# A slot of 57 columns for rows of 56: two gated 3x3 convolutions in float32 on one core

## The chip, the core and the metric

The kernel runs on one core of one Trainium2 chip. The metric is the device time of one execution in microseconds (us). The core has a matrix engine (TensorE, called PE in the profile, its weight loads PEld), a vector engine (DVE), a scalar engine (ACT), GpSimd (POOL), and SyncE (SP), which issues most of the DMAs. SBUF holds the operands, 128 partitions wide. PSUM takes the sums of TensorE, in 8 banks of 512 float32 columns.

## What is computed

The input x has 16 images, 64 channels, 56 by 56 pixels. A gated convolution with batch norm and ReLU is followed by a second one, and x is added before the last ReLU:

```python
def qconv_cg(x, w, theta):
    base = x.shape[1] // 4
    yp = conv3x3(x[:, :base], w[:, :base])        # padding 1 on each side
    yr = conv3x3(x[:, base:], w[:, base:])
    d = sigmoid(2.0 * (yp - theta[None, :, None, None]))
    return yp + d * yr
h = relu(bn(qconv_cg(x, w_a, theta_a), gamma_a, beta_a, mean_a, var_a))
h = bn(qconv_cg(h, w_b, theta_b), gamma_b, beta_b, mean_b, var_b)
return relu(x + h)
```

## The kernel before

**Layout.** Two neighbouring rows of an image share a slot: partition 2c+q holds channel c of the row of parity q. An image has 28 pairs of output rows and, since a pair of output rows reads four input rows, XS = 29 slots in the input layout. A row has W = 56 pixels, and in the tiles that TensorE reads (`x_hi`, `x_lo`, `h_hi`, `h_lo`, lines 112 to 115) it is stored with a zero on each side, so a slot takes PADW = 58 columns. The 3x3 taps become 2 slots by 3 shifts of dx = 0, 1 or 2 columns, six taps, each a 32 by 128 matrix for each of four groups of 16 channels.

**Precision.** A value is stored as a high part that TensorE's fast float32 format can hold and a low part, the rest. Each tap is done three times: high by high, high data by low weights, low data by high weights. That makes UNITS = 18 matmuls for each block and channel group.

**Blocks.** A block is BLK = 8 slots, N = 8 x 56 = 448 output columns of one PSUM bank. Convolution a has 56 blocks (the last of every seven takes 4 slots of each of two images, `a_slots`), convolution b has 58. `h_hi` and `h_lo` are rings of 116 slots, and two of the b blocks fall on the ring's end. After a lead of seven a blocks, `order` alternates b and a blocks, 114 in all.

**TensorE's work** is written out by hand in the loop at lines 324 to 362. A step issues one matmul for each of the channel groups 1, 2, 3, 0, in the order of the tuple. Each group sits in its own 32 rows of the array, so that the four run side by side. Groups 2, and 3 and 0, lag group 1 by 21 and 42 steps (LAG), so there are 18 x 114 + 42 = 2094 steps, the first and last 42 with fewer groups. Groups 1 to 3 add into one of five `yr` banks, group 0 into one of three `yp` banks (`yr_bank`, `yp_bank`, lines 175 to 179). `moving` (line 292) gives the data operand: eight rows of 56 columns out of slots of 58, shifted by dx. `unit` (line 312) issues the matmul on line 320.

**The other engines.** For each block ACT takes the sigmoid of the `yp` bank (line 403), DVE multiplies by the `yr` bank (503) and adds the `yp` bank (505). For an a block ACT then applies the batch norm and ReLU (409) and writes `h_hi` (414), DVE writes `h_lo` (510); for a b block DVE adds x (524) and ACT does the last ReLU (422). The splitting of x into `x_hi` (ACT, 378) and `x_lo` (DVE, 485) runs four a blocks ahead. At the start DVE and POOL write the zero columns and zero slots (lines 434, 263 and 266).

Of the kernel before, what the change touches and what calls it, by code (L numbers as in the profile page):

```python
# [10 lines left out]
P = 128  # L11
# [18 lines left out]
def gated_conv_pair_kernel(nc, x, w_a, theta_a, gamma_a, beta_a, mean_a, var_a,  # L30
# [4 lines left out]
    XS = SLOTS + 1  # L35
    PADW = W + 2
    N = BLK * W
    HALF = BLK // 2
    assert N <= BANK and SLOTS == 3 * BLK + HALF and (B * XS) % BLK == 0
    HRING = H_IMGS * XS  # L40
# [63 lines left out]
    with ExitStack() as ctx:  # L104
        def sb(name, shape, dt=F32):
            return ctx.enter_context(nc.sbuf_tensor(name, shape, dt))
# [4 lines left out]
        x32 = sb("x32", [P, X_IMGS * XS, W])  # L111
        x_hi = sb("x_hi", [P, XH_IMGS, XS, PADW], F32R)
        x_lo = sb("x_lo", [P, XH_IMGS, XS, PADW], F32R)
        h_hi = sb("h_hi", [P, HRING + 1, PADW], F32R)
        h_lo = sb("h_lo", [P, HRING + 1, PADW], F32R)
        mix = sb("mix", [P, MIX, N])
        rows_out = sb("rows_out", [P, OUT_IMGS * XS, W])
# [56 lines left out]

        def yr_bank(b):
            return psum[:, b % YR_BANKS, 0:N]

        def yp_bank(b):
            return psum[:, YR_BANKS + b % YP_BANKS, 0:N]

        def in_middle(tile, n):

            parts = a_slots(n)
            img, s, k = parts[0]
            t = (img % H_IMGS) * XS + 1 + s
            if len(parts) == 1:
                return tile[:, t:t + k, 1:1 + W]
            pair = tile[:, (img % H_IMGS) * XS:(img % H_IMGS + 2) * XS].rearrange("p (i s) w -> p i s w", i=2)
            return pair[:, :, 1 + s:1 + s + k, 1:1 + W]
# [12 lines left out]
        def split_chunk(tile, img, c):  # L202
            s0, s1 = CHUNKS[c]
            return tile[:, img % XH_IMGS, s0:s1, 1:1 + W]

# [46 lines left out]
        def _(pool):  # L252
# [9 lines left out]
            for n, t in enumerate((h_hi, h_lo)):  # L262
                nc.gpsimd.memset(t[:, :, 0:PADW:PADW - 1].bitcast(F32), 0.0).then_inc(hpads_zero, 1)

                pool.wait_ge(hpads_zero, 2 * n + 1)
                nc.gpsimd.memset(t[:, 0:HRING + 1:XS, :].bitcast(F32), 0.0).then_inc(hpads_zero, 1)

        @block.tensor
        def _(pe):
# [21 lines left out]

            def moving(blk, part, c, dx, g):
                kind, n = blk
                rows = slice(g * ROWS, (g + 1) * ROWS)
                if kind == "a":
                    tile = (x_hi, x_lo)[part]
                    parts = a_slots(n)
                    img, s, k = parts[0]
                    at = img % XH_IMGS
# [4 lines left out]
                t = BLK * n % HRING  # L304
                if t == HRING - HALF:
                    halves = tile[rows, c:c + HRING].rearrange("p (a b) w -> p a b w", b=HALF)
                    return halves[:, 0::HRING // HALF - 1, :, dx:dx + W]
# [57 lines left out]
        def _(act):  # L365
# [60 lines left out]
        def _(dve):  # L426
# [72 lines left out]
            for b, (kind, n) in enumerate(order):  # L499
                m = mix[:, b % MIX]  # L500
                dve.wait_ge(gate_ready, b + 1)
                dve.wait_ge(yr_ready, b + 1)
                nc.vector.tensor_tensor(m, m, yr_bank(b), ALU.mult).then_inc(gated_ready, 1)  # L503
                dve.wait_ge(gated_ready, b + 1)
                nc.vector.tensor_tensor(m, m, yp_bank(b), ALU.add).then_inc(mixed_ready, 1)  # L505
                if kind == "a":
# [46 lines left out]
```

## Time and profile before

| | us |
|---|---|
| median of 3 runs | 471.18 (470.81 to 471.21) |
| the profiled execution, its whole time | 471.88 |
| its span, from first to last instruction | 469.8 |
| PE busy, PEld busy | 452.7 (96%), 445.1 (95%) |
| DVE busy, ACT busy | 257.7 (55%), 219.6 (47%) |

Matmuls overlap one another, so PE's busy time says that some matmul was always under way, not how fast the columns flow. What tells this is the distance from the start of one matmul of a channel group to the start of the next of the same group. It is called a step below, and is read from the timeline.

### The profile page before, as it was taken

To read this page: it belongs to the slowest core of one execution; us is meant where nothing else is said; L and a number is where in the kernel's file an instruction comes from. 1 tells how busy PE (TensorE), PEld (TensorE's weight loads), DVE (VectorE), ACT (ScalarE), POOL (GpSimd) and SP (SyncE) were. 2 spreads that over 40 slices of the span, in tenths; PEclk is the share of its full clock that TensorE was granted. 3 is DMA by queue.
4 is the path that set the end of the run, shared out by engine and by line. 5 is a ranking of instruction groups with operands and counts; after the bars stand their busy time and mean duration, and the time that the engine had idled before them with its cause. 6 is when DMAs were issued, how large, how long until landed. Compare 5 with 4: busy or idle time off the path is not lost.

```text
span 469.8 us, 17744 instructions
## 1 busy us (share of the span) xinstructions
PE 452.7 (96%) x8233; PEld 445.1 (95%) x8233; DVE 257.7 (55%) x425; ACT 219.6 (47%) x346; POOL 7.0 (1%) x20
## 2 busy tenths in 40 slices
PE   3999999999999999999999999999999999999991
PEld 3999999999999999999999999999999999999991
DVE  8206655565655555565656555565656555545552
ACT  3226645454544545454544545454544545443331
POOL 5000000000000000000000000000000000000000
PEclk9999999999999999999999999999999999999996
DMA  9920000801726051070506151070333003030333
GB/s 176 218 43 3 3 3 3 137 3 26 116 44 96 3 119 22 8 135 19 122 3 117 26 117 24 4 139 1 81 62 71 3 1 71 3 66 6 72 72 68
DMA packets 116298, 27.13 MB, mean 58 GB/s; under 512 B 116096, under 2 KB 116096, under 8 KB 116224
## 3 DMA queue, kind: packets, MB, share of 16 engines
q1 hardware_dynamic: 115312, 25.86, 30.1%
q8 instruction: 65, 1.06, 1.0%
q10 hardware_dynamic: 592, 0.13, 0.1%
q14 instruction: 9, 0.07, 0.0%
q0 software_dynamic: 320, 0.00, 0.0%
HBM read 13.14 MB, written 12.85 MB: 55 GB/s over the span
## 4 chain that ended last, share of the span: by engine, by line
PE 96%; DVE 1%; ACT 1%; DMA 1%; issue 0%; ACTq 0%
PE acc L320 95%; DMA w_nat<-in_L_conv_w_a_dram 1%; DVE w_pad L441 0%; PE acc L281 0%; ACT L403 0%; ACT mix L403 0%; DVE w_lo L449 0%; ACT w_hi L369 0%; DVE rows_out L524 0%; ACT rows_out L422 0%; DVE mix L505 0%; DVE mix L503 0%; DVE x_lo L485 0%; ACT x_hi L378 0%; PE acc L289 0%
## 5 line engine op out<-in xcount | busy, mean ns | idle before, releaser
L320 PE MATMUL acc<-h_hi,w_hi 32*128 32x448 f32 x1392 | 226.7, 367 | 0.0
L320 PE MATMUL acc<-h_lo,w_hi 32*128 32x448 f32 x1392 | 226.6, 367 | 0.0
L320 PE MATMUL acc<-h_hi,w_lo 32*128 32x448 f32 x1392 | 226.5, 367 | 0.0
L320 PE MATMUL acc<-x_hi,w_hi 32*128 32x448 f32 x1344 | 224.5, 374 | 0.1
L320 PE MATMUL acc<-x_lo,w_hi 32*128 32x448 f32 x1344 | 224.2, 372 | 0.0
L320 PE MATMUL acc<-x_hi,w_lo 32*128 32x448 f32 x1344 | 224.1, 373 | 0.0
L320 PEld LDWEIGHTS acc<-h_hi,w_hi 32*128 32x128 f32 x1392 | 188.3, 184 | 1.2
L320 PEld LDWEIGHTS acc<-h_hi,w_lo 32*128 32x128 f32 x1392 | 188.2, 183 | 1.2
L320 PEld LDWEIGHTS acc<-h_lo,w_hi 32*128 32x128 f32 x1392 | 188.2, 183 | 1.0
L320 PEld LDWEIGHTS acc<-x_hi,w_hi 32*128 32x128 f32 x1344 | 185.9, 188 | 1.4 <-ACT x_hi L378 0.4
L320 PEld LDWEIGHTS acc<-x_hi,w_lo 32*128 32x128 f32 x1344 | 186.1, 188 | 1.0
L320 PEld LDWEIGHTS acc<-x_lo,w_hi 32*128 32x128 f32 x1344 | 185.9, 187 | 1.0
L503 DVE TENSOR_TENSOR mix<-mix,acc 128x448 f32<-128x448 f32 x114 | 70.8, 621 | 142.1 <-ACT mix L403 142.1
L422 ACT ACTIVATE rows_out<-rows_out,shift 128x448 f32<-128x448 f32 (+3 forms) x64 | 40.0, 634 | 120.4 <-DVE rows_out L524 120.4
L403 ACT ACTIVATE mix<-acc,gate_bias 128x448 f32<-128x448 f32 x114 | 72.3, 634 | 45.1 <-PE acc L320 44.4
L505 DVE TENSOR_TENSOR mix<-mix,acc 128x448 f32<-128x448 f32 x114 | 70.7, 620 | 3.9
L409 ACT ACTIVATE mix<-mix,shift,inv 128x448 f32<-128x448 f32 x56 | 42.7, 762 | 51.2 <-DVE mix L505 51.2
L510 DVE TENSOR_TENSOR h_lo<-mix,h_hi 128x448 fp32r<-128x448 f32 x56 | 35.1, 626 | 52.9 <-ACT h_hi L414 52.9
L524 DVE SCALAR_TENSOR_TENSOR rows_out<-mix,inv,x 128x448 f32<-128x448 f32 (+3 forms) x64 | 40.5, 641 | 2.0
L485 DVE TENSOR_TENSOR x_lo<-x,x_hi 128x504 fp32r<-128x504 f32 (+2 forms) x48 | 34.3, 715 | 1.3 <-ACT x_hi L378 1.3
L414 ACT ACTIVATE h_hi<-mix 128x448 fp32r<-128x448 f32 x56 | 32.5, 581 | 1.8
L378 ACT ACTIVATE x_hi<-x 128x504 fp32r<-128x504 f32 (+2 forms) x48 | 31.1, 649 | 2.5 <-DMA x<-in_x_dram 2.4
(47 smaller groups left out, 29.9 us busy)
## 6 DMA issues: line engine op xcount, KB each, us to landing
out_dram<-rows_out SPq DMA_DIRECT2D x32, 392.0 KB, 6.7
x<-in_x_dram SPq DMA_DIRECT2D x30, 392.0 KB, 5.5
x<-in_x_dram SPq DMA_DIRECT2D x1, 280.0 KB, 4.7
x<-in_x_dram SPq DMA_DIRECT2D x1, 266.0 KB, 5.1
w_nat<-in_L_conv_w_a_dram SPq DMA_DIRECT2D x1, 144.0 KB, 2.9
w_nat<-in_L_conv_w_b_dram SPq DMA_DIRECT2D x1, 144.0 KB, 4.0
x<-in_x_dram ACTq DMA_DIRECT2D x1, 126.0 KB, 3.0
x<-in_x_dram SPq DMA_DIRECT2D x1, 112.0 KB, 4.0
```

What stands on the lines that cost most here:

```text
L320: return pe.matmul(psum[:, bank, 0:N], w[g * ROWS:(g + 1) * ROWS, tap], moving(blk, part, c, dx, g), start=(u == 0 and g in (0, 1)), stop= ...
L378: nc.scalar.activation(split_chunk(x_hi, img, c), x_chunk(img, c), ACT.Copy).then_inc(xhi_ready, 1)
L403: nc.scalar.activation(mix[:, b % MIX], yp_bank(b), ACT.Sigmoid, scale=ALPHA, bias=gate_bias[:, k:k + 1]).then_inc(gate_ready, 1)
L409: nc.scalar.activation(mix[:, b % MIX], mix[:, b % MIX], ACT.Relu, scale=inv[:, 0:1], bias=shift[:, 0:1]).then_inc(h_ready, 1)
L414: nc.scalar.activation(in_middle(h_hi, n), as_block(mix[:, b % MIX], n), ACT.Copy).then_inc(hhi_ready, 1)
L422: last = nc.scalar.activation(rows, rows, ACT.Relu, bias=shift[:, 1:2])
L485: nc.vector.tensor_tensor(split_chunk(x_lo, img, c), x_chunk(img, c), split_chunk(x_hi, img, c).bitcast(F32), ALU.subtract).then_inc(xlo_r ...
L503: nc.vector.tensor_tensor(m, m, yr_bank(b), ALU.mult).then_inc(gated_ready, 1)
L505: nc.vector.tensor_tensor(m, m, yp_bank(b), ALU.add).then_inc(mixed_ready, 1)
L510: nc.vector.tensor_tensor(in_middle(h_lo, n), as_block(m, n), in_middle(h_hi, n).bitcast(F32), ALU.subtract).then_inc(hlo_ready, 1)
L524: last = nc.vector.scalar_tensor_tensor(rows_out[:, at:at + s, :].rearrange("p s w -> p (s w)"), m[:, col:col + s * W], inv[:, 1:2], x32[: ...
```

## The change

A row is now stored with one zero ahead of it, PITCH = 57 columns to a slot, and the zero ahead of the next slot's row serves as the one behind. A spare column stands ahead of the first slot and one behind the last. The data operand of a matmul is then SPAN = 8 x 57 = 456 columns in one run (for the blocks of two images and those on the ring's end, two runs of 228). The sums take 456 columns of a bank; column 0 of each slot's 57 is a sum that nobody needs, and ACT and DVE read the 56 behind it. The number of matmuls, their order, waits, banks and lags stay. Of the zeroing instructions, the one for two columns of each slot becomes one for the spare column and one for a column of each slot.

```diff
-    PADW = W + 2
-    N = BLK * W
+    PITCH = W + 1
+    SPAN = BLK * PITCH
...
+    def b_slots(m):
+        t = BLK * m % HRING
+        return [(0, HALF), (t, HALF)] if t == HRING - HALF else [(t, BLK)]
...
-        x_hi = sb("x_hi", [P, XH_IMGS, XS, PADW], F32R)
-        h_hi = sb("h_hi", [P, HRING + 1, PADW], F32R)
+        x_hi = sb("x_hi", [P, XH_IMGS, 1 + XS * PITCH + 1], F32R)
+        h_hi = sb("h_hi", [P, 1 + (HRING + 1) * PITCH + 1], F32R)
...
-        def yr_bank(b):
-            return psum[:, b % YR_BANKS, 0:N]
+        def slots(tile, t, k):
+            return tile[:, 1 + t * PITCH:1 + (t + k) * PITCH].rearrange("p (s w) -> p s w", w=PITCH)
+        def rows_of(bank):
+            return psum[:, bank, 0:SPAN].rearrange("p (s w) -> p s w", w=PITCH)[:, :, 1:]
...
-                    if len(parts) == 1:
-                        return tile[rows, at, s + c:s + c + k, dx:dx + W]
-                    return tile[rows, at:at + 2, s + c:s + c + k, dx:dx + W]
+                    at = (s + c) * PITCH + dx
+                    if len(parts) == 1:
+                        return tile[rows, img % XH_IMGS, at:at + SPAN]
+                    return tile[rows, img % XH_IMGS:img % XH_IMGS + 2, at:at + HALF * PITCH]
...
-                return tile[rows, t + c:t + c + BLK, dx:dx + W]
+                    return tile[rows, at:at + SPAN]
...
-                return pe.matmul(psum[:, bank, 0:N], w[g * ROWS:(g + 1) * ROWS, tap],
+                return pe.matmul(sums(bank, blk), w[g * ROWS:(g + 1) * ROWS, tap],
...
-                nc.scalar.activation(mix[:, b % MIX], yp_bank(b), ACT.Sigmoid, scale=ALPHA,
+                nc.scalar.activation(mix_rows(b), yp_rows(b), ACT.Sigmoid, scale=ALPHA,
...
-                last = nc.vector.memset(t[:, :, :, 0:PADW:PADW - 1].bitcast(F32), 0.0)
+                nc.vector.memset(t[:, :, 0].bitcast(F32), 0.0)
+                last = nc.vector.memset(t[:, :, 1::PITCH].bitcast(F32), 0.0)
...
-                nc.vector.tensor_tensor(m, m, yr_bank(b), ALU.mult).then_inc(gated_ready, 1)
+                nc.vector.tensor_tensor(mix_rows(b), mix_rows(b), yr_rows(b), ALU.mult).then_inc(gated_ready, 1)
```

## Rows read from the trace of the kernel before

**Rows 1.** The page, busy time of each engine: us (share of span) xinstructions.
```profile
PE 452.7 (96%) x8233; PEld 445.1 (95%) x8233; DVE 257.7 (55%) x425; ACT 219.6 (47%) x346; POOL 7.0 (1%) x20
```
**Rows 2.** The chain that ended last: start us, us, what.
```profile
10.63 21.57 PE acc L320 x126
...
34.71 425.35 PE acc L320 x7317
...
460.09 0.64 ACT mix L403
```
**Rows 3.** The page's costliest groups, line 320: busy us, mean ns of one.
```profile
L320 PE MATMUL acc<-h_hi,w_hi 32*128 32x448 f32 x1392 | 226.7, 367 | 0.0
...
L320 PEld LDWEIGHTS acc<-h_hi,w_hi 32*128 32x128 f32 x1392 | 188.3, 184 | 1.2
```
**Rows 4.** Timeline of PE, first stage, one group, then four: start us, us, engine, operation.
```profile
13.58 1.69 PE L320 MATMUL acc<-x_hi,w_lo 32*128 32x448 f32 x4
15.07 1.69 PE L320 MATMUL acc<-x_lo,w_hi 32*128 32x448 f32 x4
...
29.26 0.62 PE L320 MATMUL acc<-x_lo,w_hi 32*128 32x448 f32 x2
...
29.63 0.62 PE L320 MATMUL acc<-x_lo,w_hi 32*128 32x448 f32 x2
```
**Rows 5.** Two stretches: busy us (xinstructions) of each engine, granted clock, DMA, GB/s.
```profile
10.50:30.60 20.10, 20.10 (x118) 19.17 (x122) 4.52 (x16) 2.87 (x5) 0.00 (x0) 1.00 0.98 166
...
35.90:450.80 414.90, 414.90 (x7900) 409.79 (x7896) 236.77 (x381) 205.38 (x325) 0.00 (x0) 1.00 0.26 49
```
**Rows 6.** Timeline of PE near the end, three groups active, then two.
```profile
450.84 1.20 PE L320 MATMUL acc<-h_lo,w_hi 32*128 32x448 f32 x12
...
452.10 1.20 PE L320 MATMUL acc<-h_hi,w_hi 32*128 32x448 f32 x12
...
456.06 1.44 PE L320 MATMUL acc<-h_hi,w_hi 32*128 32x448 f32 x12
457.33 1.44 PE L320 MATMUL acc<-h_hi,w_lo 32*128 32x448 f32 x12
```
**Rows 7.** Timeline of PE in the middle, four steps on end, all four groups active.
```profile
200.16 0.38 PE L320 MATMUL acc<-h_hi,w_lo 32*128 32x448 f32 x2
...
200.37 0.38 PE L320 MATMUL acc<-h_hi,w_lo 32*128 32x448 f32 x2
...
200.58 0.38 PE L320 MATMUL acc<-h_hi,w_lo 32*128 32x448 f32 x2
...
200.78 0.38 PE L320 MATMUL acc<-h_hi,w_lo 32*128 32x448 f32 x2
```
**Rows 8.** Timeline of PE where group 1 begins its fifth block.
```profile
34.71 0.47 PE L320 MATMUL acc<-x_hi,w_hi 32*128 32x448 f32 x1
...
35.03 0.36 PE L320 MATMUL acc<-x_hi,w_hi 32*128 32x448 f32 x1
```
**Rows 9.** Timeline of the weight loads (PEld) there, with idle time before and its releaser.
```profile
34.71 0.18 PEld L320 LDWEIGHTS acc<-x_hi,w_hi 32*128 32x128 f32 x1 [0.45 <-ACT x_hi L378]
...
34.82 0.18 PEld L320 LDWEIGHTS acc<-x_hi,w_hi 32*128 32x128 f32 x1
```
**Rows 10.** Groups of instructions by shape, ACT and DVE: busy us, mean ns | idle before.
```profile
L378 ACT ACTIVATE x_hi<-x 128x672 fp32r<-128x672 f32 x16 | 12.1, 758 | 0.0
...
L378 ACT ACTIVATE x_hi<-x 128x448 fp32r<-128x448 f32 x16 | 9.1, 571 | 0.1
...
L485 DVE TENSOR_TENSOR x_lo<-x,x_hi 128x672 fp32r<-128x672 f32 x16 | 13.6, 851 | 0.0
...
L485 DVE TENSOR_TENSOR x_lo<-x,x_hi 128x448 fp32r<-128x448 f32 x16 | 9.9, 618 | 0.0
```
**Rows 11.** Waits in 35.9 to 450.8 us: who waited for whom, us, times, longest.
```profile
DVE mix L503 <- ACT mix L403: 119.5, 108, 1.8
...
ACT mix L403 <- PE acc L320: 43.2, 102, 0.5
```

More of the change, by code:

```diff
@@ L35, in gated_conv_pair_kernel @@
     XS = SLOTS + 1
-    PADW = W + 2
-    N = BLK * W
+    PITCH = W + 1
     HALF = BLK // 2
-    assert N <= BANK and SLOTS == 3 * BLK + HALF and (B * XS) % BLK == 0
+    SPAN = BLK * PITCH
+    assert SPAN <= BANK and SLOTS == 3 * BLK + HALF and (B * XS) % BLK == 0
     HRING = H_IMGS * XS
@@ L111, in gated_conv_pair_kernel @@
         x32 = sb("x32", [P, X_IMGS * XS, W])
-        x_hi = sb("x_hi", [P, XH_IMGS, XS, PADW], F32R)
-        x_lo = sb("x_lo", [P, XH_IMGS, XS, PADW], F32R)
-        h_hi = sb("h_hi", [P, HRING + 1, PADW], F32R)
-        h_lo = sb("h_lo", [P, HRING + 1, PADW], F32R)
-        mix = sb("mix", [P, MIX, N])
+        x_hi = sb("x_hi", [P, XH_IMGS, 1 + XS * PITCH + 1], F32R)
+        x_lo = sb("x_lo", [P, XH_IMGS, 1 + XS * PITCH + 1], F32R)
+        h_hi = sb("h_hi", [P, 1 + (HRING + 1) * PITCH + 1], F32R)
+        h_lo = sb("h_lo", [P, 1 + (HRING + 1) * PITCH + 1], F32R)
+        mix = sb("mix", [P, MIX, BLK * W])
         rows_out = sb("rows_out", [P, OUT_IMGS * XS, W])
@@ L173, in gated_conv_pair_kernel, with yr_rows, yp_rows, mix_rows @@
         out_stored = [sem(f"out_stored{n}") for n in range(OUT_IMGS)]
-        def yr_bank(b):
-            return psum[:, b % YR_BANKS, 0:N]
-        def yp_bank(b):
-            return psum[:, YR_BANKS + b % YP_BANKS, 0:N]
+        def slots(tile, t, k):
+            return tile[:, 1 + t * PITCH:1 + (t + k) * PITCH].rearrange("p (s w) -> p s w", w=PITCH)
+        def rows_of(bank):
+            return psum[:, bank, 0:SPAN].rearrange("p (s w) -> p s w", w=PITCH)[:, :, 1:]
+        def yr_rows(b):
+            return rows_of(b % YR_BANKS)
+        def yp_rows(b):
+            return rows_of(YR_BANKS + b % YP_BANKS)
+        def mix_rows(b):
+            return mix[:, b % MIX].rearrange("p (s w) -> p s w", w=W)
         def in_middle(tile, n):
@@ L186, in in_middle @@
             if len(parts) == 1:
-                return tile[:, t:t + k, 1:1 + W]
-            pair = tile[:, (img % H_IMGS) * XS:(img % H_IMGS + 2) * XS].rearrange("p (i s) w -> p i s w", i=2)
+                return slots(tile, t, k)[:, :, 1:1 + W]
+            pair = slots(tile, (img % H_IMGS) * XS, 2 * XS).rearrange("p (i s) w -> p i s w", i=2)
             return pair[:, :, 1 + s:1 + s + k, 1:1 + W]
@@ L203, in split_chunk @@
             s0, s1 = CHUNKS[c]
-            return tile[:, img % XH_IMGS, s0:s1, 1:1 + W]
+            return slots(tile[:, img % XH_IMGS], s0, s1 - s0)[:, :, 1:1 + W]
         block = ctx.enter_context(nc.Block())
@@ L262, in _ @@
             for n, t in enumerate((h_hi, h_lo)):
-                nc.gpsimd.memset(t[:, :, 0:PADW:PADW - 1].bitcast(F32), 0.0).then_inc(hpads_zero, 1)
+                nc.gpsimd.memset(t[:, 0:1].bitcast(F32), 0.0)
+                nc.gpsimd.memset(t[:, 1::PITCH].bitcast(F32), 0.0).then_inc(hpads_zero, 1)
                 pool.wait_ge(hpads_zero, 2 * n + 1)
-                nc.gpsimd.memset(t[:, 0:HRING + 1:XS, :].bitcast(F32), 0.0).then_inc(hpads_zero, 1)
+                nc.gpsimd.memset(slots(t, 0, HRING + 1)[:, 0:HRING + 1:XS, :].bitcast(F32), 0.0
+                                 ).then_inc(hpads_zero, 1)
         @block.tensor
@@ L298, in moving, with sums @@
                     img, s, k = parts[0]
-                    at = img % XH_IMGS
+                    at = (s + c) * PITCH + dx
                     if len(parts) == 1:
-                        return tile[rows, at, s + c:s + c + k, dx:dx + W]
-                    return tile[rows, at:at + 2, s + c:s + c + k, dx:dx + W]
+                        return tile[rows, img % XH_IMGS, at:at + SPAN]
+                    return tile[rows, img % XH_IMGS:img % XH_IMGS + 2, at:at + HALF * PITCH]
                 tile = (h_hi, h_lo)[part]
[L304 to L307, printed above, removed]
-                return tile[rows, t + c:t + c + BLK, dx:dx + W]
+                parts = b_slots(n)
+                at = (parts[0][0] + c) * PITCH + dx
+                if len(parts) == 1:
+                    return tile[rows, at:at + SPAN]
+                halves = tile[rows, at:at + HRING * PITCH].rearrange("p (i w) -> p i w", w=HALF * PITCH)
+                return halves[:, 0::HRING // HALF - 1, 0:HALF * PITCH]
+            def sums(bank, blk):
+                kind, n = blk
+                if len(a_slots(n) if kind == "a" else b_slots(n)) == 1:
+                    return psum[:, bank, 0:SPAN]
+                return psum[:, bank, 0:SPAN].rearrange("p (i w) -> p i w", i=2)[:, :, 0:HALF * PITCH]
             UNITS = 2 * TAPS * 3
@@ L502, in _ @@
                 dve.wait_ge(yr_ready, b + 1)
-                nc.vector.tensor_tensor(m, m, yr_bank(b), ALU.mult).then_inc(gated_ready, 1)
+                nc.vector.tensor_tensor(mix_rows(b), mix_rows(b), yr_rows(b), ALU.mult).then_inc(gated_ready, 1)
                 dve.wait_ge(gated_ready, b + 1)
-                nc.vector.tensor_tensor(m, m, yp_bank(b), ALU.add).then_inc(mixed_ready, 1)
+                nc.vector.tensor_tensor(mix_rows(b), mix_rows(b), yp_rows(b), ALU.add).then_inc(mixed_ready, 1)
                 if kind == "a":
```

## Prediction, made before the change was run

> **What bounds the kernel now.** I read the page first. TensorE is busy 96% of the span, DVE 55%, ACT 47% [rows 1]. The chain of waits agrees: matmuls of line 320 hold it from 10.63 us on, are left once for ACT's work before 34.71 us, and then hold it for 425.35 us without a break, until ACT, DVE and a store finish the last block [rows 2]. Between 35.9 and 450.8 us ACT waits 43.2 us for TensorE's sums, and DVE waits for ACT, 119.5 us [rows 11]; no row there has TensorE waiting. So the time is the number of steps times the length of a step, and the question is what makes a step as long as it is.
>
> A step is read from the timeline as the distance between starts. In the middle stretch 7900 matmuls, four to a step, take 414.9 us: 414.9 / 1975 = 210.1 ns a step [rows 5]. That is more than the columns need. TensorE has two clock levels, 1.2 and 2.4 GHz; the granted clock reads 1.00 in this stretch, the upper one, and 448 columns at 2.4 GHz are 186.7 ns. **So 23.4 ns of every step are something else than columns.** In the first 20 us a step is 373 ns (four steps from 13.58 to 15.07 us; 0.37 us from 29.26 to 29.63), with one group active as with four [rows 4]. That is 448 / 1.2 = 373.3 ns, the lower clock, although the granted-clock column reads 1.00 there too [rows 5]; I trust the step. At that clock nothing is on top of the columns. The extra thus isn't work of the array itself, which would cost at either clock, but of something that feeds it and is hidden when the array takes its columns at half speed.
>
> What can it be? Three things can be put aside. **Not the issue of instructions**: with four groups a step has eight (four loads, four matmuls), near the end three groups have six and two have four, and six steps there take 1.26 us and 1.27 us, still 210 to 212 ns [rows 6]. **Not a wait for weights**: where TensorE had been idle, load and matmul start together at 34.71 us, and that matmul takes 0.47 us instead of 0.37 [rows 8, 9] (367 ns is the usual mean [rows 3]), so the weights were usable after some 0.10 us; the next load starts at 34.82 us, and the matmul that needs it could have started at about 34.92, but it starts at 35.03 [rows 8, 9]. (The 184 ns that the page gives for a load [rows 3] is longer than what the matmul waited for.) **Not the alignment of a row's start**: the shift dx goes 0, 1, 2 from step to step, the same in all four groups since their lags are multiples of three, and three steps on end take 0.21, 0.21 and 0.20 us [rows 7]. What is left is a cost per run of columns (eight rows, eight restarts of the address in each matmul), or a cost per matmul.
>
> The Trainium skill (Advanced Engine Details and Errata, Memory Cachelines) says that SBUF is read in lines of 16 bytes, that each change of line has a penalty unless it is absorbed, and that access patterns with gaps slow matmuls a lot, the latter of PSUM. A row of 56 columns that starts off a line touches 15 lines in place of 14, which would make a step depend on dx; the rows above show no such dependence, so the trace does not bear out the lines as the cause, though it leaves the gaps.
>
> **The change, part by part.** *Columns*: 456 in place of 448 cost 8 / 2.4 = 3.3 ns a step at the upper clock and 8 / 1.2 = 6.7 ns at the lower, where rows 4 show that time goes exactly by columns. *Runs*: eight become one. No row shows a matmul of one run at the upper clock, so the cost of a run is bounded from both sides by rows 4 and 5. At most all the 23.4 ns belong to the seven gaps, and a step becomes 190.0 ns; at the other end none does, and a step becomes 190.0 + 23.4 = 213.4 ns. I take it that each run has the same cost, 23.4 / 8 = 2.9 ns, whether it begins a matmul or a row in it. The reason is the first stage: a restart of the address is just such a thing as runs ahead unseen at 1.2 GHz and shows at 2.4, and it does not depend on dx, the number of groups or the tile. One run is then left: **190.0 + 2.9 = 192.9 ns a step**, 17.2 ns less than 210.1.
>
> *Steps from 34.71 us on*: group 1 begins its fifth block there, at step 72 of 2094, so 2022 steps are left; 2022 x 210.1 = 424.8 us, which is the chain's 425.35 [rows 2]. They save 2022 x 17.2 = 34.8 us. The clock rises after some 54 steps; the 18 steps between save 18 x 17.2 = 0.3 us.
>
> *First stage*: the 54 steps at the lower clock take 6.7 ns more each, 0.36 us. If the clock rises at the same moment, one step less is done by then and is made up at the upper clock: 0.2 us lost.
>
> *The stall at 34.71 us*: group 1's fifth block waits for a piece of `x_hi`, which ACT splits off after the first block's sigmoid, and PEld idles 0.45 us [rows 9]. ACT's chain there doesn't get shorter. From the end of the first block to this point TensorE has 12 steps, which become 12 x 17.2 = 0.2 us shorter, so that the stall grows by as much: 0.2 us lost.
>
> *Blocks of two runs*: eight a blocks on two images and two b blocks on the ring's end keep one gap, 2.9 ns. Since the three lags spread a block's 18 steps over 18 + 42 = 60, some group is in such a block in up to 10 x 54 = 540 steps; 540 x 2.9 = 1.6 us if the slowest group sets the step, 180 x 2.9 = 0.5 us if the groups run on their own. I take 1.0 us.
>
> *ACT and DVE* now read and write rows with gaps where they had one run. The splits into the padded tiles show what a row costs there: ACT takes 758 ns for 12 rows of 56 and 571 for 8, or 187 / 224 = 0.83 ns a column, DVE 233 / 224 = 1.04 ns [rows 10], with nothing left over for the four more rows that exceeds one column's time each. So I put it at 0 for eight rows, between a gain of nothing and 8 ns for each of five instructions of a block. It lies beside TensorE's work save in the last block, where 3 x 8 ns are lost at most. With a pair of blocks (36 steps) down from 7.56 to 6.94 us, DVE's load in the middle stretch goes from 236.8 / 414.9 = 57% to 62%, ACT's from 49 to 54% [rows 5]: neither becomes the bound. A `yp` bank must be free two blocks after its last sum, 6.9 us, and sigmoid, product and sum need about 2 us. *Zeroing*: it moves as many columns with four more short instructions, on POOL and on DVE ahead of its wait for the weights; I put it at 0 us, since DVE then waits for the weights in any case; at worst two more of its mean instructions, 2 x 257.7 / 425 = 1.2 us [rows 1]. *DMA*: its mean share in the middle stretch is 0.26 [rows 5] and it may be asked for 8% sooner; 0 us.
>
> **Sum.** 34.8 + 0.3 - 0.2 - 0.2 - 1.0 = 33.7 us saved. The profiled execution took 471.88 us (span 469.8), so it becomes 438.2. The median of the runs is 0.7 us below the profiled one, hence 437.5 us.
>
> **Rivals.**
> 1. *A cost per matmul* (the slower side). The 23.4 ns belong to the handing over from one matmul of a group to the next, and the gaps cost nothing. For it: that too would be hidden at 1.2 GHz, and would not depend on dx or the number of groups. Also, a matmul takes 570 ns in the first stage (four that start 373 ns apart span 1.69 us, and 1.69 - 3 x 0.373 = 0.57 [rows 4]) and 367 later [rows 3], so 197 ns beyond the columns, then 180 if no gap is within it, or 157 if all are: the nearer agreement is without gaps. Against it: the ends of matmuls are modelled, and weights are ready early. Price: 3.3 ns x 2040 steps = 6.8 us, 0.2 us in the first stage: 471.2 + 7.0 = 478.2 us. It decides as soon as fewer than 3.3 of the 23.4 ns, 14%, belong to the gaps. A rate of delivery that makes every column 9/8 as long (210.0 ns for 448) comes out beside it: 213.8 ns, 479 us.
> 2. *A part of it*: the gaps hold half, a step becomes 190.0 + 11.7 = 201.7 ns, and the saving is 2040 x 8.4 - 1 = 16 us: 455 us; the case reaches from 444 to 468.
> 3. *The change doesn't shorten the step*: something of fixed length (a load with what follows it) sets 210 ns whatever the columns do. Only the first stage pays, 0.2 us: 471.4 us. Rows 8 and 9 speak against it.
>
> The Trainium skill (TensorE: Matmul & The Clock Gate, Back-to-back issue gap) gives N / 2.4 + 2.5 ns for a matmul behind another at the upper clock and N / 1.2 at the lower, and says elsewhere on that page that throughput is purely the number of columns. The lower clock agrees with rows 4; for the upper one it would give 189.2 ns now, where rows 5 give 210.1, so the rule leaves out what this case turns on. By it the changed step would be 192.5 ns, and by its slope alone, with today's extra kept, the first rival's 213.4.
>
> **How the numbers follow.** The step at a cost per run: 0.47, **437.5 us**, own range 431 (step 190.0: 2.9 x 2040 = 5.9 us less) to 444. A part: 0.15. No shorter step: 0.08, 471.4. Slower: 0.30, 478 to 479. A measurement tells 0.2%, about 1 us, from no change, so faster has 0.62, same 0.08, slower 0.30. To leave out no more than 2 in 10 the range must take in the slower case: 431 to 479.
>
> **What would show it.** In the changed profile the middle stretch gives the step: near 193 ns if each run costs, 190 if only gaps do, 213 if it is per matmul. The steps of the first stage must read 380 ns. If gaps lie inside a matmul, its mean of 367 ns falls, to about 350; if it rises by 3 ns, the first rival holds. Blocks of two runs should show steps a few ns longer than others. The prediction is wrong if the step stays over 196 ns, if TensorE waits for `yp` or `yr` banks, or if PEld idles at more places than before.

## The result, and the profile after

The changed kernel takes 467.55 us (467.38 to 468.12, 4 runs) against 471.19 (470.81 to 471.67) for the kernel before: a ratio of 0.9924, 95% interval 0.9907 to 0.9941. It is faster by 3.6 us, where 33.7 were forecast. The time lies in the range that was given (431 to 479) only because that range had to take in the slower rival; the likeliest case's own range, 431 to 444, missed it by far.

The page of the changed kernel, busy times and one group of line 350 (320 before): us, mean ns of one.

```profile
span 465.3 us, 17748 instructions
PE 447.9 (96%) x8233; PEld 441.8 (95%) x8233; DVE 257.8 (55%) x427; ACT 219.6 (47%) x346; POOL 6.8 (1%) x22
...
L350 PE MATMUL acc<-h_hi,w_hi 32*128 32x456 f32 x1392 | 224.2, 365 | 0.0
```

Its chain of waits: start us, us, what.

```profile
10.88 21.02 PE acc L350 x122
...
34.42 421.14 PE acc L350 x7300
...
455.58 0.64 ACT mix L433
```

Against [rows 1, 3] the shape of the profile is the same. The whole difference is in the long piece of the chain: 425.35 us before [rows 2], 421.14 now. Both cover steps 72 to 2093, 2022 of them, so a step has gone **from 210.4 to 208.3 ns** and not to 192.9. The pieces before and behind it are nearly as they were: it starts at 34.42 against 34.71 us, and the span ends 9.7 us behind it in both. In what follows a kernel's step is this piece of its chain divided by 2022. In three pairs of kernels below that differ only in their first 42 steps the piece is the same to 0.01 us.

Taken apart, a step of the kernel before was 186.7 ns of columns and 23.7 more; now it is 190.0 and 18.3. Where do the 18.3 come from, and are the 5.4 that went the gaps' share?

### The profile page after: what moved, and what is told of

It is laid out like the page before. It is cut to its first block, busy times and chain, and to the rows that moved or that the text cites. A ratio compares the mean times of both kernels' runs of the same rounds, so it can differ in the third digit from the quotient of the medians.

```text
span 465.3 us, 17748 instructions
## 1 busy us (share of the span) xinstructions
PE 447.9 (96%) x8233; PEld 441.8 (95%) x8233; DVE 257.8 (55%) x427; ACT 219.6 (47%) x346; POOL 6.8 (1%) x22
## 4 chain that ended last, share of the span: by engine, by line
PE 95%; DVE 2%; ACT 1%; DMA 1%; issue 0%; ACTq 0%
PE acc L350 95%; DVE w_pad L472 1%; DMA w_nat<-in_L_conv_w_a_dram 1%; ACT L433 0%; ACT mix L433 0%; DVE w_lo L480 0%; DVE rows_out L555 0%; ACT rows_out L452 0%; DVE mix L534 0%; DVE mix L536 0%; DVE x_lo L516 0%; ACT x_hi L408 0%; DVE w_pad L469 0%; PE acc L310 0%; DVE prm_dup L524 0%
## 5 line engine op out<-in xcount | busy, mean ns | idle before, releaser
L350 PE MATMUL acc<-h_hi,w_lo 32*128 32x456 f32 x1392 | 224.4, 365 | 0.0
L350 PE MATMUL acc<-h_lo,w_hi 32*128 32x456 f32 x1392 | 224.2, 365 | 0.0
L350 PE MATMUL acc<-h_hi,w_hi 32*128 32x456 f32 x1392 | 224.2, 365 | 0.0
L350 PE MATMUL acc<-x_hi,w_hi 32*128 32x456 f32 x1344 | 222.0, 372 | 0.1
L350 PE MATMUL acc<-x_hi,w_lo 32*128 32x456 f32 x1344 | 221.3, 370 | 0.0
L350 PE MATMUL acc<-x_lo,w_hi 32*128 32x456 f32 x1344 | 220.9, 368 | 0.0
```

The lines of the kernel that those rows point to most:

```text
L350: return pe.matmul(sums(bank, blk), w[g * ROWS:(g + 1) * ROWS, tap], moving(blk, part, c, dx, g), start=(u == 0 and g in (0, 1)), stop=(u ...
```

## Experiment 1: one run of 448 columns

The last 8 of the 456 columns are left out of every matmul, so that against the kernel before only the gaps and the slots' width differ, and against the changed one only the columns.

```diff
-                        return tile[rows, img % XH_IMGS, at:at + SPAN]
+                        return tile[rows, img % XH_IMGS, at:at + BLK * W]
...
-                    return psum[:, bank, 0:SPAN]
+                    return psum[:, bank, 0:BLK * W]
```

> The changed kernel with each matmul streaming only the first 448 of its 456 columns (224 of 228 where there are two runs); the last columns of each block are left out of the sums. Against the changed kernel it takes away 8 columns and no gap, against the kernel before it takes away seven gaps and no column. The changed kernel's step is 208.1 ns, 190.0 of columns and 18.1 beyond. Theory A, the rest is a fixed cost per matmul: step 186.7 + 18.1 = 204.8 ns, 467.5 - 3.3 x 2.04 = 460.8 us. Theory B, the rest is a rate (each column 1.095 times its 1 / 2.4 ns): 204.4 ns, 460.1 us. Theory C, something else of fixed length sets about 208 ns (a weight load and what follows it): step 208, 467.5 us.

Measured: 460.07 us, 0.9747 (0.9727 to 0.9767) of the kernel before. The chain's long piece:

```profile
34.50 413.76 PE acc L350 x7650
```

413.76 / 2022 = 204.6 ns. Eight columns cost 208.3 - 204.6 = 3.7 ns a step and 7.5 us in all, a little more than their 3.3 ns at 2.4 GHz. Theory C, a fixed length, falls; A and B (204.8 and 204.4 ns) are too near each other here.

## Experiment 2: matmuls alone, by length, format and gaps

To find what a step is made of I ran kernels that hold nothing but matmuls in stages. They copy x into a float32 tile of TensorE's fast format (`xr`) and a bfloat16 tile (`xb`), and each stage has 60 steps of four matmuls, one for each group of 32 rows, on a line of its own:

```python
for r in range(R):                 # R = 60
    for g in (1, 2, 3, 0):
        pe.matmul(psum[:, g, 0:456], W(xr, g, r), flat(xr, g, r % 3, 456), **fl(r))
```

> A kernel of matmuls alone, which leaves the convolutions out: copies of x as data and weights, then stages of 60 steps, four matmuls a step in four groups of 32 rows unless said, each stage on its own line. What is read is the step, from the first and last start of the line. Theory A (18 ns a matmul): 456 columns 208, 448 in one run 205, 512 231, 384 178, 320 151, 256 125, 128 71 ns. Theory B (a rate of 1.095): 208, 204, 234, 175, 146, 117, 58. Theory C (a floor near 208): 208 for all up to 456, 231 or less at 512. The gaps: 8 runs of 56 should give 210, as in the kernel before; if a gap costs 0.8 ns, 19 runs of 24 give 208 + 14 = 222 and 57 runs of 8 give 208 + 43 = 251; if it costs a part of a line instead, the short runs cost more. What the fixed part hangs on: if it is the adding into the same bank, matmuls that take banks in turn lose it (190); if it is the weights' change, 64 columns of weights or the same weights again lose a part; if it is the four bytes of a column, bfloat16 data lose it (190 to 192); if it is the four groups side by side, one group alone or one matmul on all 128 rows loses it. If none does, it belongs to every matmul behind another.

The chain of waits of this kernel: start us, us, what. A stage's us divided by 60 is its step.

```profile
41.29 12.53 PE acc L78 x240
53.83 12.33 PE acc L83 x235
66.16 12.53 PE acc L88 x240
78.69 13.87 PE acc L93 x239
92.56 10.60 PE acc L98 x238
103.16 8.89 PE acc L103 x239
112.05 7.07 PE acc L108 x238
119.12 6.65 PE acc L113 x239
125.77 12.58 PE acc L118 x240
...
150.88 12.40 PE acc L128 x239
163.28 11.58 PE acc L133 x240
174.86 11.75 PE acc L138 x240
```

| line | stage | step, ns | beyond columns / 2.4 |
|---|---|---|---|
| 78 | 456 columns, one run | 208.8 | 18.8 |
| 83 | 448, one run | 205.5 | 18.8 |
| 88 | 448 as 8 runs of 56 in slots of 58 | 208.8 | 22.2 |
| 93 | 512, one run | 231.2 | 17.8 |
| 98, 103, 108 | 384, 320, 256 | 176.7, 148.2, 117.8 | 16.7, 14.8, 11.2 |
| 113 | 128 | 110.8 | 57.5 |
| 118 | 456, banks in turn | 209.7 | 19.7 |
| 128 | 456, weights of 64 columns | 206.7 | 16.7 |
| 133 | 456, bfloat16 | **193.0** | 3.0 |
| 138 | 456, bfloat16, 8 runs of 57 in slots of 58 | 195.8 | 5.8 |
| 153 | 456 as 19 runs of 24 in slots of 25 | 215.9 | 25.9 |
| 158 | 456 as 57 runs of 8 in slots of 9 | 229.6 | 39.6 |
| 168 | 448 read in one run, summed into 8 runs of 56 in slots of 58 | 205.5 | 18.8 |

(The last three are read from the first and last start of their lines, by which line 78 gives 208.9.)

The kernel's step is here without any other engine: 208.8 ns for one run, and 448 columns in eight runs cost 3.4 ns more than in one, **0.5 ns a gap and not 2.9**. The 18 gaps of line 153 cost 7.0 ns and the 56 of line 158 20.7, 0.4 ns each; gaps in the sums cost nothing (line 168). What is beyond the columns is neither a fixed cost per matmul (it falls from 18.8 to 11.2 ns between 448 and 256 columns) nor quite a rate (it doesn't grow from 448 to 512). It is not the adding into one bank (line 118, which includes the first steps after a change of banks, is no faster), and weights of half the columns take off only 2 ns. What does take it off is bfloat16: 3.0 ns are left. At 128 columns another floor shows, 111 ns, in the fast float32 format (224 columns took 112 ns in experiment 5's kernel). The same data and weights in every step gave 205.6 ns and matmuls on all 128 rows at once 208.8, so the four groups side by side are not it either.

A gap of one column costs about what reading that column would. The 474 columns that line 153 spans from first to last lie between 456 and 480 in one run (208.9 and 218.9 ns, the latter in experiment 3's kernel), which gives 216.4 ns for 474, an estimate, against 215.9; line 158 spans 512 and takes 229.6 against the 231.2 of line 93.

The stage with one group alone went another way: its step rose from 0.21 to 0.38 us after 14 steps, and the clock fell with it. Two stretches of line 143, busy us, granted clock behind POOL's:

```profile
186.30:189.20 2.90, 2.90 (x22) 2.57 (x15) 0.00 (x0) 0.00 (x0) 0.00 (x0) 1.00 0.00 0
189.30:205.70 16.40, 16.40 (x44) 14.09 (x44) 0.00 (x0) 0.00 (x0) 0.00 (x0) 0.50 0.01 1
```

A granted clock of 0.50 is the lower level, 1.2 GHz, given 3 us after the one group was left alone at 186.3 us (experiment 7's expectation says 4). The stage of two runs behind it (line 148) began at that clock and is not used; those behind that ran at the upper one. Experiment 7 comes back to this.

## Experiment 3: weights, start, gaps and slots

> Matmuls alone again, the convolutions left out, in stages on lines of their own. The stages before gave steps of 208.9 ns for 456 columns, 205.5 for 448, 231.1 for 512, 176.8 for 384, 148.3 for 320 and 117.8 for 256, that is 18.9, 18.8, 17.8, 16.8, 14.9 and 11.1 ns beyond the columns at 2.4 GHz, and 192.8 for bfloat16 (2.8 beyond). Theory D: a float32 load of weights, under way for the first 180 ns or so of a step, slows the data by a tenth, so the rest grows with the columns up to some 440 and then stays. Then 480 columns give 218.8; weights of 32 columns, whose load is shorter (130 ns at 64 columns against 183 at 128), give at most 190 + 10 = 200, and weights of 96 some 207.5. Theory E: the data themselves, four bytes a column, come a tenth late, whatever the load: weights of 32 columns stay at 206 or more. Both give bfloat16 at 512, 256 and 128 columns 2.8 ns beyond the columns: 216.1, 109.5, 56.1. Where the run starts (column 0, 1 or 2) should matter by 1 to 3 ns, since the same address each time gave 205.6. A gap, by the stages before, costs 3.4 / 7 = 0.5 ns: two runs of 228 then 209.4, four of 112 207.0, eight of 56 in slots of 57, 58, 60 or 64 208.9 each; if it is a matter of where a row starts in memory, slots of 60 and 64 differ from those of 57 and 58. Two groups instead of four: 208.9, if the clock holds.

The chain of waits; the stages are 456 columns from column 0, 1 and 2 (lines 78, 83, 88), weights of 32 columns (98), eight runs of 56 in slots of 57, 58, 60 and 64 (113 to 128).

```profile
40.52 12.27 PE acc L78 x238
52.79 12.60 PE acc L83 x240
65.39 12.41 PE acc L88 x238
...
90.20 12.41 PE acc L98 x240
...
115.23 12.47 PE acc L108 x236
127.70 12.47 PE acc L113 x234
140.17 12.54 PE acc L118 x240
152.71 12.80 PE acc L123 x240
165.50 12.67 PE acc L128 x240
```

Three readings. The load is not it: with weights of 32 columns a step still takes 206.8 ns, so theory D, which asked for 200 at most, falls. **The start counts**: 204.5, 210.0 and 206.8 ns from column 0, 1 and 2. And **the slot's width counts**: 207.8, 209.0, 213.3 and 211.2 ns for 57, 58, 60 and 64, with the same number of gaps and columns. So a wider gap is cheaper than its columns would be: slots of 64 span 504 columns, and 480 in one run already take 218.9 ns. (Line 108, four runs of 112, 207.8; line 103, two runs of 228, 210.4.) In bfloat16, 512, 256 and 128 columns took 216.1, 109.4 and 56 ns, all three near the expected 2.8 beyond the columns. The stage of 128 has two halts in it, which its mean must leave out: one step of 0.26 us, and one of 2 us in which TensorE waited for nothing that the profile shows:

```profile
210.68 3.52 PE L148 MATMUL acc<-xb 32*128 32x128 bf16 x223
215.95 0.41 PE L148 MATMUL acc<-xb 32*128 32x128 bf16 x16 [1.75 <-issue]
```

All its other steps are 55 to 58 ns. Two groups at full clock took 104 ns for each of two matmuls, 209 a step.

## Experiment 4: the slots' width in the kernel

Two kernels undo or push one part. The first keeps slots of 57 and goes back to eight runs of 56, summed into 448 columns without gaps:

```diff
-                    return tile[rows, at:at + SPAN]
+                    return tile[rows, at:at + SPAN].rearrange("p (s w) -> p s w", w=PITCH)[:, :, 0:W]
```

> The changed kernel's slots of 57 columns with the matmuls of the kernel before: eight runs of 56 columns, 448 in all, written in one run, and read by ACT and DVE in one run. It undoes the unbroken run and keeps the narrower slots. Theory A', the gaps alone make the difference between 210.2 ns (the kernel before) and 204.8 (448 columns in one run), 0.8 ns a gap: step 210.2, 471.5 us. Theory F, the width of the slot (where the rows start in memory) makes some of it: a step of 205 to 209, 461 to 469 us.

Measured: **466.48 us**, 0.990 (0.988 to 0.992). The second is the kernel before with slots of 60:

```diff
-    PADW = W + 2
+    PADW = W + 4
```

> The kernel before with slots of 60 columns in place of 58, two of them unused; matmuls of eight runs of 56 as before. If only the number of gaps counts (theory A'): step 210.2, 471.3 us. If it counts where the rows start (theory F, by which 57 gave 208.1 and 58 gives 210.2 in the kernels, and 207.7, 208.9, 213.2 for 57, 58, 60 in the stages of matmuls alone): 213 to 215 ns, 477 to 481 us.

Measured: 474.30 us, 1.0062 (1.0044 to 1.008). The chain's long piece of the first and of the second:

```profile
33.59 420.52 PE acc L342 x7659
```

```profile
34.26 428.32 PE acc L320 x7607
```

They are 208.0 and 211.8 ns. So theory F holds and A' does not: narrower slots alone, with every gap kept, give a step of 208.0 against 210.4, and wider ones 211.8, though less than the 213 to 215 that I expected. The 210.4 to 208.3 ns of the change are the sum of three:

| part | from, to (ns a step) | difference |
|---|---|---|
| slots of 58 to slots of 57 | 210.4, 208.0 | -2.4 |
| seven gaps closed | 208.0, 204.6 | -3.4 |
| 448 to 456 columns | 204.6, 208.3 | +3.7 |

The unbroken run and its 8 columns cancel, as the stages have it: eight runs in slots of 57 span 455 columns, and that takes what 456 columns in one run take (208.0 and 208.3 ns here, 207.8 and 208.8 in the stages). What the change gained came with the narrower slots, and the kernel that has only these is 1 us faster than the changed one, 0.6 us of it in this piece (420.52 against 421.14).

The timeline of PE in the kernel with slots of 60, one step to a row, shows what the equal steps of the kernel before had hidden:

```profile
199.89 0.38 PE L320 MATMUL acc<-h_hi,w_hi 32*128 32x448 f32 x1
...
200.11 0.36 PE L320 MATMUL acc<-h_hi,w_hi 32*128 32x448 f32 x1
...
200.31 0.37 PE L320 MATMUL acc<-h_hi,w_hi 32*128 32x448 f32 x1
...
200.52 0.38 PE L320 MATMUL acc<-h_hi,w_hi 32*128 32x448 f32 x1
```

0.22, 0.20, 0.21 us: over the whole trace the shifts of 0, 1 and 2 take 204, 210 and 221 ns here (the first row has a shift of 2). In slots of 58 the rows of one matmul start at different places by turns, and the three shifts take the same [rows 7].

## Experiment 5: is it the delivery of the data's bytes?

If the bytes are the limit, bfloat16 data read 4 bytes apart must be as slow as float32.

```python
xb[32 * g:32 * g + 32, r % 3:r % 3 + 2 * 456:2]     # line 78; step 4 on line 83
xr[32 * g:32 * g + 32, r % 3:r % 3 + 2 * 456:2]     # line 93
```

> Matmuls alone, the convolutions left out, stages on lines of their own. Known by now: 456 float32 columns in one run take 204.4, 210.0 and 206.7 ns when they start at column 0, 1 and 2, weights of 32 to 96 columns take only 2.2 ns off, bfloat16 takes 192.8; eight runs of 56 take 207.7, 208.9, 213.2 and 210.9 in slots of 57, 58, 60 and 64. Theory E1: what float32 costs on top is the memory's delivery, by the address lines a column run touches. Then bfloat16 data read every second element (4 bytes apart, as float32) take about 207 instead of 193, every fourth more still; float32 every second element too; and the cost has a period of 4 columns in the start (3 near 1 or 2, 4 as 0, 5 as 1). Theory E2: it is the float32 arithmetic or format. Then bfloat16 at any distance stays near 193, and float32 every second element near 208. Slots of 61 and 65 should be as good as those of 57, 62 and 66 as 58, 59 and 63 unknown, if only the remainder by 4 counts.

```profile
41.20 12.14 PE acc L78 x238
53.34 24.20 PE acc L83 x239
77.54 11.57 PE acc L88 x240
89.11 24.20 PE acc L93 x238
```

bfloat16 packed took 193.0 ns; 4 bytes apart it takes 202.3, 8 bytes apart 403.3, and float32 8 bytes apart 403.3 as well. (Line 88 is bfloat16 with the weights spread: 192.8, no matter.) So theory E1 holds in the main: **the step follows how far apart the columns lie in memory, not the format**. E1 expected about 207 ns for the first of these; 202.3 is what float32 takes from its best starts (203.3 below). 456 columns at 8 bytes are 228 pieces of 16 bytes, 403.3 / 228 = 1.77 ns each; at 4 bytes 114 pieces would be 201.8 ns. Float32 columns in one run thus come at 0.44 ns each where the array could take one in 0.42, and what is left over, 1 to 11 ns for one run, goes with where it starts.

That last part I could not bring under a rule. I expected a period of 4 columns; the stages with runs from column 3, 4 and 5 gave 203.3, 213.3 and 213.3, and slots of 59, 61, 63 and 65 all 213.3, which says no to "the remainder by 4". With the weights in a tile of their own:

> Matmuls alone, the convolutions left out, stages on lines of their own, weights in a tile of their own and the data's first column the same in every step and group. So far: 16 bytes, four float32 columns, seem to be delivered in some 1.77 ns at best: bfloat16 read 4 bytes apart takes 202.3 ns for 456 columns and 403.3 read 8 bytes apart, float32 read 8 bytes apart 403.3. For one run of 456 from column 0 to 5 I had 204.4, 210.0, 206.7, 203.3, 213.4, 213.3, with the weights in the data's own tile. Theory G: only the pieces of 16 bytes that a run touches count (114 from column 0, 115 from others): period 4, 204.4 at 0, 4 and 8 and about 206 elsewhere; the 213 at column 4 then came from the weights' tile. Theory H: larger pieces count as well, or the distance to the weights: other values at 4 than at 0, with period 8 if at all. For eight runs of 56 in slots of 60 the kernel with such slots gave 204.3, 210.4 and 221 ns for its three shifts; from columns 0 to 4 the stages should give the same sequence, and what the fourth residue costs. Slots of 58 from column 0 and 1: a mean of residues 0 and 2, 1 and 3: 212 and 210 or so.

The chain, for 456 columns from column 0 to 8:

```profile
42.16 12.40 PE acc L80 x240
54.56 12.71 PE acc L85 x240
67.26 12.40 PE acc L90 x240
79.67 12.20 PE acc L95 x240
91.87 12.31 PE acc L100 x237
104.18 12.80 PE acc L105 x240
116.97 12.20 PE acc L110 x240
129.18 12.20 PE acc L115 x240
141.37 12.41 PE acc L120 x236
```

206.7, 211.8, 206.7, 203.3, 205.2, 213.3, 203.3, 203.3 and 206.8: column 8 is as column 0 and column 4 is not, which fits a period of 8 columns, 32 bytes, as theory H has it, and not G's of 4; it is one pair. The values moved with the weights' place too (column 0 gave 204.5 before and 206.7 here, column 4 213.3 and 205.2). In the kernel the try to use this failed:

```diff
-        x_hi = sb("x_hi", [P, XH_IMGS, XS, PADW], F32R)
+        x_hi_all = sb("x_hi", [P, 4 + XH_IMGS * XS * PADW], F32R)
```

The slots begin at column 3 of this tile.

> The kernel before with slots of 60 columns (474.3 us, shifts 204.3, 210.4 and 221 ns) and three spare columns ahead of the first slot, so that the rows of the three shifts start at residues 3, 0 and 1 of four columns in place of 0, 1 and 2. If the residue sets the step, two shifts give 204 and 210 and the third what residue 3 costs; if that is 210, as slots of 58 hint, the mean is 208.3 and the time 474.3 - 3.7 x 2.04 = 466.8 us. If not the residue but the shift itself counts, 474.3 us.

Measured: 471.66 us, 1.0003 (0.9994 to 1.0013), the three shifts 217, 204 and 210 ns where 210, 204 and 210 were expected. The place does change the time, by 2.6 us against the same slots without it. In these two kernels the remainder by 4 even orders the shifts: 0 and 1 cost 204 and 210 ns in both, 2 and 3 cost 221 and 217. But it is no rule. In the stages the same slots took 206.7, 213.3, 217.3, 213.3 and 200.3 ns from columns 0 to 4, so that column 4 isn't as column 0, and slots of 57, whose rows start at all four remainders, take 208.0 ns in the kernel where the mean of the four values is 213.

## Experiment 6: bfloat16 in the kernel

The proof in the kernel itself is to halve the bytes. The parts of data and weights are stored as bfloat16, which rounds them more coarsely; every instruction stays.

```diff
-F32R = mybir.dt.float32r
+BF16 = mybir.dt.bfloat16
...
-        x_hi = sb("x_hi", [P, XH_IMGS, 1 + XS * PITCH + 1], F32R)
+        x_hi = sb("x_hi", [P, XH_IMGS, 1 + XS * PITCH + 1], BF16)
```

> The changed kernel with the high and low parts of data and weights stored as bfloat16 in place of TensorE's float32 format: half the bytes a column, every instruction the same in number, order and columns, the parts rounded more coarsely. By the stages of matmuls alone (456 columns in one run: 192.8 ns in bfloat16, 204 to 213 in float32) the step falls from 208.1 to 192.8 ns: 467.5 - 15.3 x 2.04 = 436.3 us, the time that the prediction named for the changed kernel. If the step in the kernel is set by something else than the delivery of data (theory C, a fixed length), 467 us.

Measured: **436.94 us**, 0.9266 (0.9252 to 0.928). The same for the kernel before:

> The kernel before (eight runs of 56 in slots of 58) with the parts stored as bfloat16, rounded more coarsely. Against the run above it says what the change would be worth where the delivery of bytes is no bound. By the stages a gap costs 0.44 ns there: 186.7 + 2.8 + 7 x 0.44 = 192.6 ns a step, 471.3 - 17.6 x 2.04 = 435.4 us, so the change would be worth nothing in bfloat16 (0 to 1 us slower). If a gap costs what the prediction gave it, 2.9 ns: 186.7 + 23.4 = 210 ns, no gain over the kernel before, 471 us.

Measured: **432.78 us**, 0.9175 (0.916 to 0.9191). And for slots of 57 with eight runs:

> Slots of 57 columns, eight runs of 56, with the parts stored as bfloat16, rounded more coarsely. In bfloat16, eight runs in slots of 58 took 188.9 ns a step where the shift is 0 or 2 and 195 to 196 where it is 1, 191.9 in the mean (432.8 us), one run of 456 in slots of 57 took 193.4 (436.9 us). If it is an odd start of two bytes a column that costs 7 ns, in slots of 57 half the rows of every matmul have it, and each shift costs about the same, 192.5 ns: 434 us. If the narrower slots help in themselves, as in float32 (2.1 ns), 190 ns, 429 us.

Measured: 435.14 us, 0.9225 (0.9209 to 0.924). The long piece of the chain in the three, in this order, then the page's busy times of the first:

```profile
34.09 390.63 PE acc L350 x7115
```

```profile
33.28 387.46 PE acc L320 x7206
```

```profile
34.61 389.66 PE acc L342 x7694
```

```profile
PE 416.9 (96%) x8233; PEld 223.5 (51%) x8233; DVE 257.7 (59%) x427; ACT 218.2 (50%) x346; POOL 7.5 (2%) x22
```

The steps are 193.2, 191.6 and 192.7 ns. With half the bytes, the changed kernel comes to the step and the time that the prediction named for float32, 192.9 ns and 437.5 us. That is a coincidence, for the kernel before comes lower still: all 23 ns but 5 go without a single gap closed. There the change as a whole is a loss, 1.6 ns a step and 4.2 us, and its narrower slots alone lose 1.1 ns: in slots of 58 the shifts of 0 and 2 take 188.8 and 189.8 ns and only the odd one 196, while slots of 57 put an odd start into every matmul (192 to 193 ns for each shift). So in bfloat16 gaps between rows that start on 4 bytes cost next to nothing. That the float32 excess is in the main the delivery of the data's bytes is shown, by this and by experiment 5 together: here the format changes with the bytes, and the loads shorten too (PEld from 95% to 51% busy), but experiment 5 had brought 9.5 of the 16 ns between the formats back in bfloat16 by spacing alone, and experiment 3 had ruled out the loads as the main cause.

## Experiment 7: fewer steps at the lower clock

The first 42 steps have one or two groups at work, and the first 20 us run at the lower clock. In experiment 2 one group alone lost the upper clock. If the clock follows how many groups are at work, matmuls that only fill the idle groups should bring it up sooner.

```diff
+            FILLERS = {2: (0, 7), 3: (0, 6), 0: (14, 5)}
...
+                    if step < LAG[g]:
+                        mm = pe.matmul(psum[:, bank, 0:SPAN], w_hi[0][g * ROWS:(g + 1) * ROWS, step % 6],
+                                       moving(("a", 0), 0, 0, step % TAPS, g), start=True, stop=True)
```

`FILLERS` has, for each group, the first step that is filled and a bank that is free then.

> The changed kernel with filling matmuls in the first 42 steps: where groups 2, 3 and 0 still wait for group 1's first block, they multiply data nobody needs into banks 7, 6 and 5 that are free then (116 more matmuls or so). In the stages of matmuls alone a single group of 32 rows was given the lower clock about 4 us after it was left alone, its step rose from 209 to 380 ns, and four groups brought the upper clock back; in the kernel before and in the changed one the first 20 us have one or two groups and steps of 373 and 380 ns. If the clock follows how much of the array is busy, it rises some 5 us after the first matmul, at about 16 us in place of 30, and 14 us at 380 ns a step, 37 steps, take 37 x 208 = 7.7 us: 467.5 - 6.5 = 461 us. If it rises by time since something else, or if the fillers get in the way, 467.5 us or more.

Measured: **461.38 us**, 0.9795 (0.9774 to 0.9817). Timeline of PE, group 1's matmuls on line 351:

```profile
14.08 0.58 PE L351 MATMUL acc<-x_hi,w_lo 32*128 32x456 f32 x1
...
14.46 0.58 PE L351 MATMUL acc<-x_hi,w_lo 32*128 32x456 f32 x1
...
15.42 0.36 PE L351 MATMUL acc<-x_lo,w_hi 32*128 32x456 f32 x1
...
15.62 0.36 PE L351 MATMUL acc<-x_lo,w_hi 32*128 32x456 f32 x1
```

The step falls from 0.38 to 0.20 us at about 15 us, in place of 30, with 91 fillers. So the time until the rise follows what is at work, and is no fixed time from the first matmul. On slots of 57 with eight runs:

> Slots of 57 columns with eight runs of 56 (466.5 us by itself) and the filling matmuls of the first 42 steps (worth 6.2 us on the changed kernel, 467.55 to 461.38). If the two add: 466.5 - 6.2 = 460.3 us. If the fillers' gain was in part the 8 columns at the lower clock (380 against 373 ns a step), a few tenths less: 460.6.

Measured: 460.68 us, 0.9775 (0.9761 to 0.979). And on the kernel before with bfloat16 parts:

> The kernel before with bfloat16 parts, rounded more coarsely (432.8 us), and the filling matmuls of the first 42 steps, worth 6.2 us on the changed kernel and 5.8 us on the one with eight runs of 57. A step at the lower clock is 373 ns as before, one at the upper 192, so that the clock's rise 14 us earlier is worth a little more: 432.8 - 6.5 = 426.3 us. If four groups that read two bytes a column do not bring the clock up so early, less.

Measured: **426.98 us**, 0.9052 (0.9038 to 0.9066), the fastest of all. Of the kernels with float32 parts that compute the whole result, the two above are the fastest, both ahead of the changed kernel by over 6 us.

## Why the prediction was wrong

**The bound and the way to read it: right.** The chain, the share of TensorE and a step of 210 ns against 186.7 ns of columns were what the time turns on, and 2022 steps times the step's change, 2022 x 2.1 = 4.2 us, is what the chain lost (3.6 us by the medians). Of the three causes put aside, two stayed aside: the issue of instructions (the same 8233 matmuls in bfloat16 take 193 ns a step) and the wait for weights (206.8 ns with weights of 32 columns). The third, the alignment of a row's start, did not.

**The step that failed is the choice of what is left.** "What is left is a cost per run of columns, or a cost per matmul": the list was not complete. A limit on the delivery of float32 bytes is hidden at 1.2 GHz just as well, and it had been named only as a fixed 9/8 beside the first rival. From there "each run has the same cost" gave the seven gaps 20.5 ns; they measured 3.4, 0.5 ns each, in the kernel as in the stages, and the 8 columns took them back. The term 2022 x 17.2 = 34.8 us was in truth 2022 x 2.1. What stands in its place is the delivery of the float32 data: 193.2 ns a step with half the bytes against 208.3, 202.3 in bfloat16 spread to 4 bytes a column.

**"Not the alignment of a row's start" was a wrong reading.** Three equal steps [rows 7] only say that in slots of 58 the three shifts cost the same, since eight rows start at several remainders at once. Slots of 60 have shifts from 204 to 221 ns. The 2.4 ns that the narrower slots gave, which is all of the change's net gain of 2.1, had no term in the sum at all. That the gain is there at all is thus not what the prediction had reckoned with. The Trainium skill (Advanced Engine Details and Errata, Memory Cachelines) had spoken of 16-byte lines in SBUF and of a penalty for changing them; I turned that down on the strength of rows 7. Runs with data 8 bytes apart, two columns to a line, took 403.3 ns for 456 columns against 193 packed in bfloat16, so lines matter here, and two uses of a line, which that section calls enough to absorb the latency, are not enough at 2.4 GHz. How starts count is not in it.

**The rivals.** The first, a cost per matmul, falls: bfloat16 leaves 2.8 to 3.0 ns in the stages and 3.2 in the kernel with one run. That is the rule of the Trainium skill (TensorE: Matmul & The Clock Gate, Back-to-back issue gap), N / 2.4 + 2.5 ns, which the trace agrees with in bfloat16 (192.8, 216.1 and 56 ns at 456, 512 and 128 columns) and not in float32 (208.8 at 456). The second, a part of it, had the right kind of outcome but not the mechanism: 467.5 is at the very end of its 444 to 468. Its parts were -3.4 for the gaps and +3.7 for the columns, near the break-even point of 14% that I had worked out for the first rival (3.4 of 23.7 is 14%), which makes the unbroken run worth nothing. The third, no shorter step, was the nearest in time (471.4), but 448 columns took 3.7 ns less than 456, so no fixed length sets the step.

**The small terms held.** ACT's and DVE's instructions on rows with gaps took 636, 622 and 621 ns against 634, 621 and 620; steps of the first stage took 380 ns; PEld idled 0.5 us at the one known place of the loop and nowhere else in it. The steps with some group in a block of two runs were no longer than the others (208.2 and 208.1 ns), so the term of 1.0 us for them was nothing. The mean matmul went from 367 to 365 ns and not to 350, which was named as the sign that the gaps aren't in it.

**What stays open** is the rule by which the start of a run or row sets a float32 step between 200 and 221 ns, and its part in the excess that grows with the columns from 11.2 ns (256) to 18.8 (448).

## What to carry to other kernels

Before a gap, a wait or a fixed cost is blamed for time beyond the columns, halve the bytes of the data in a small kernel of matmuls alone: in the fast float32 format columns come slower than the array takes them at 2.4 GHz, and only what remains in bfloat16 may be the instruction's own. Compare layouts by their slot width with everything else held, since here one column of width gave 2.4 ns a step where the unbroken run with its columns gave nothing, and a mean over shifts can hide differences of 16 ns. In float32, padding columns that only join runs are paid in full (3.7 ns for 8) and a gap of one column costs as much (3.4 ns for 7), so closing such gaps by reading them gains nothing. Wider gaps cost less than their columns would.

## What was new of the hardware

- Four groups of 32 rows, or one matmul on all 128, kept the upper clock, and two groups did for the 12 us of their stage (step 209 ns); one group alone, always busy, was given 1.2 GHz after 3 us (granted clock 0.50, step 0.38 us). Filling the idle groups for 42 steps was worth 6.2 us here.
- Data columns 4 bytes apart arrive at 0.44 ns a column (202.3 ns for 456 in bfloat16 spread), 8 bytes apart at 0.88 (403.3, in float32 and bfloat16 alike).
- A float32 matmul of 128 or 224 columns came every 111 or 112 ns, one of 128 columns in bfloat16 every 56.
- Gaps in the sums' bank cost nothing (205.5 ns for 448 columns in 8 runs, 205.6 in one); one-column gaps in the float32 data cost 0.4 to 0.5 ns each, as much as a column.
